# Four-layer attention and expert kernel: the first layer's gate in fewer operations, its row index from two small one-hot tables

## The reference, cut to what matters

```python
K = sigmoid(decay)                                  # attention
states = scan(s = K * s + (kv @ W_in.T + b_in))
y = Z + mean(states @ W_out.T + b_out)
x += (y - mean(y)) / sqrt(var(y) + eps) * gamma + beta

logits = h @ gate_w.T                               # experts
scores = sqrt(softplus(logits))
_, topk_idx = top_k(scores + bias, 6)
topk_w = 1.5 * normalised(scores at topk_idx)
pos = cumsum(onehot(topk_idx)) - 1                  # place in the expert; over 95: dropped
xb[eid, pos] = h
y = (silu(xb @ w_gate) * (xb @ w_up)) @ w_down * topk_w
x += sum of a token's y + shared expert
```

## Time and profile before

| | us |
|---|---|
| median of 3 runs | 1120.19 |
| lowest, highest | 1115.52, 1121.29 |
| the profiled execution | 1117.14 |
| its span (first to last instruction) | 1115.8 |
| mean granted TensorE clock, share of full | 0.948 |
| TensorE busy | 973.4 (87%) |
| VectorE busy | 760.2 (68%) |
| ScalarE busy | 636.0 (57%) |
| GpSimd busy | 532.6 (48%) |

### The profile page before, as it was taken

One profiled execution on the slowest core, in us unless ns is written; L12 is line 12 of the kernel. 1 busy time (PEld: TensorE's weight loads), 2 busy tenths in 40 slices (PEclk: granted clock), 3 DMA queues, 4 the chain that ended last, 5 costly groups with the idle time before them and its releaser, 6 DMA issues.

```text
span 1115.8 us, 18204 instructions
## 1 busy us (share of the span) xinstructions
PE 973.4 (87%) x5865; PEld 797.3 (71%) x5865; DVE 760.2 (68%) x2009; ACT 636.0 (57%) x1808; POOL 532.6 (48%) x584
## 2 busy tenths in 40 slices
PE   5898987189998877769999999999999989998897
PEld 4674654146686656668888888888888778676785
DVE  5685222375657347778899889888987688767344
ACT  2432542002134436759898989899988754653353
POOL 3703677245545363324555555444553145453453
PEclk9788999599998899989999999999999989998999
DMA  9401887830004863020102020101000063005674
GB/s 388 165 12 34 221 210 180 247 78 1 1 1 166 289 218 132 1 61 2 63 1 63 1 63 1 63 1 62 1 24 2 1 202 71 1 1 203 229 273 160
DMA packets 57550, 108.60 MB, mean 97 GB/s; under 512 B 13872, under 2 KB 35504, under 8 KB 55536
## 3 DMA queue, kind: packets, MB, share of 16 engines
q1 hardware_dynamic: 48208, 89.44, 24.1%
q0 software_dynamic: 9248, 18.00, 6.2%
HBM read 78.67 MB, written 27.42 MB: 95 GB/s over the span
## 4 chain that ended last, share of the span: by engine, by line
PE 46%; DVE 20%; ACT 14%; issue 7%; POOL 6%; DMA 5%; SPq 1%; ACTq 0%; DVEq 0%; POOLq 0%
PE bank L200 23%; PE bank L209 8%; ACT a_p L3027 4%; ACT a_p L3035 3%; PE bank L1296 2%; PE bank L2577 2%; DMA sum<-f_ys,f_index 2%; PE bank L1830 2%; ACT a_qt L3010 2%; POOL f_xs L2148 2%; DVE a_qn L2786 2%; DVE stats L239 1%; ACT a_p L2977 1%; PE bank L2627 1%; DVE a_top L2810 1%
## 5 line engine op out<-in xcount | busy, mean ns | idle before, releaser
L3154 POOL TENSOR_TENSOR a_p<-a_p,a_tot 128x128 f32<-128x128 f32 x64 | 50.6, 809 | 183.7 <-DVE a_tot L2758 183.7
L200 PE MATMUL bank<-a_w_high,a_in 128*128 128x256 f32 x384 | 99.0, 295 | 13.8 <-ACT a_p L3035 5.0
L209 PE MATMUL bank<-const 128*128 128x128 f32 x457 | 65.4, 303 | 43.2 <-DVE x L1073 21.7
L200 PE MATMUL bank<-a_w_low,a_in 128*128 128x256 f32 x384 | 94.5, 284 | 0.0
L209 PEld LDWEIGHTS bank<-const 128*128 128x128 f32 x457 | 59.6, 158 | 47.9 <-DVE x L1073 22.1
L200 PEld LDWEIGHTS bank<-a_w_high,a_in 128*128 128x128 f32 x384 | 73.9, 192 | 16.2 <-ACT a_kx L3004 5.5
L3027 ACT ACTIVATE a_p<-bank,a_top 128x256 f32<-128x256 f32 x128 | 59.2, 480 | 31.1 <-DVE a_top L2810 28.7
L200 PEld LDWEIGHTS bank<-a_w_low,a_in 128*128 128x128 f32 x384 | 74.0, 193 | 0.0
L2810 DVE TENSOR_REDUCE a_top<-bank 128x2 f32<-128x512 f32 (+1 forms) x96 | 57.2, 601 | 20.4 <-PE bank L2577 15.7
L200 PE MATMUL bank<-cols,a_kv 128*128 128x256 f32 x256 | 61.9, 384 | 3.6 <-ACT a_kv L2950 3.6
L200 PE MATMUL bank<-a_proj_high,a_catq 128*128 128x256 f32 x256 | 62.2, 284 | 1.2 <-DVE a_catq L2205 0.8
(11 more groups left out here) (437 smaller groups left out, 3087.1 us busy)
## 6 DMA issues: line engine op xcount, KB each, us to landing
experts<-in_experts SPq DMA_DIRECT2D x49, 384.0 KB, 4.5
f_expert<-in_experts SPq DMA_DIRECT2D x31, 384.0 KB, 4.8
third_shelf<-in_groups SPq DMA_DIRECT2D x8, 1024.0 KB, 6.9
f_got<-f_xs SPq DMA_DIRECT2D x10, 516.0 KB, 8.0
third_shelf<-in_groups SPq DMA_DIRECT2D x8, 512.0 KB, 4.2
f_got<-f_ys SPq DMA_DIRECT2D x8, 512.0 KB, 5.1
f_xs<-blank_zero SPq DMA_DIRECT2D x1, 3999.0 KB, 20.8
l_expert<-in_experts SPq DMA_DIRECT2D x10, 384.0 KB, 7.5
```

Source lines behind the costliest of these rows:

```text
L200: ins = pe.matmul(out, lhs, rhs, start=start and n == 0, stop=stop and n == len(pairs) - 1, skip_group_check=shared)
L209: ins = k.pe.transpose(o, i, ident[0:i.shape[0], 0:i.shape[0]])
L3154: g_.tensor_tensor(cross_probs(m, ti), cross_probs(m, ti), over(m.tot[n % 2][:, first:first + HPG], SC), ALU.mult).then_inc(*s["cross_weig ...
```

## The change

In the attention ScalarE makes the sigmoid first, VectorE adds beta itself (two operations over four tiles each, one ahead of `l_keeps` and one after the mean) and finishes all eight tiles; GpSimd is left with the two powers. In the experts' front the rows are shared with ScalarE as in the attention. TensorE does 28 dummy transposes ahead of the turn, 10 instead of 64 behind the key products, and 18 between the place products and the index products as before. ScalarE calls Ln once on one column ahead of the gate's logits, and its four fold copies all come behind the real Ln. The correction of the logarithm is now additive and lies beside ScalarE's Ln. `root_vector` has one Newton step and one step of a higher order, and gives the root itself but for a factor. The mask comes from `max`, a copy of two large values into places 7 and 8 of the best eight, `match_replace`, and one comparison.

The place is held as `code`, the count plus 8 for a chosen expert and 0 for the others, in 16 bits, and split into `low` (three bits) and `high`. Two one-hot tables are compared from them, `low_hot` (32 groups of 8 x 8, 2048 elements) and `high_hot` (32 groups of 12 x 8, 3072 elements). `facts` is `low_hot` times the token's number in two parts, one scaled on VectorE in one operation and one on ScalarE in eight. TensorE multiplies `high_hot` with `facts` in 32 products of 128 columns into one bank; VectorE keeps the diagonal, eight more products with `spread` bring it to 96 x 32, twice, and one reduction makes `number`. The eight grids, the six copies and the table's DMA are gone. The shared expert waits for the index at its third step only. AHEAD is 14, and in GpSimd's loop the scatter now comes ahead of the gather.

```diff
 def layer0_attention_vector(k, m, s, s2):
     normalise_vector(k, s, k.x, k.rows, k.x_ready)
+    def add_beta(half):
...
+        v.tensor_tensor(k.x[:, part, :], k.x[:, part, :], under(w["beta"], HALF), ALU.add).then_inc(*step.one())
+    add_beta(0)
     on.wait_ge(*s["gained"].at(1))
...
+    add_beta(1)
...
-        for c in VECTOR_TILES:
+        for c in range(HALF):
 def layer0_attention_scalar(k, m, s):
-    normalise_scalar(k, s, k.x, k.rows, k.x_ready)
     on.wait_ge(*k.l0_in)
     a.activation(m.keep[:], w["decay"], ACT.Sigmoid).then_inc(*s["gained"].one())
+    normalise_scalar(k, s, k.x, k.rows, k.x_ready)
 def layer0_ffn_tensor(k, m, s):
+    pass_time(k, k.bank[0], 28)
+    turn_rows_tensor(k, s, k.rows, rows_of(s))
...
-    pass_time(k, k.bank[4], 64)
+    pass_time(k, k.bank[4], 10)
     on.wait_ge(*s["mask_ready"].at(1))
...
+    pass_time(k, k.bank[1], 18)
+    on.wait_ge(*s["hot_ready"].at(2))
+    for i in range(NT):
+        on.wait_ge(*s["facts_scaled"].at(i + 1))
+        for c in range(OF):
+            n = i * OF + c
+            ins = pe.matmul(counts[:, c, :], m.high_hot[:, n, :, :].rearrange("p h e -> p (h e)"),
+                            m.facts[:, n, :, :, :].rearrange("p f l e -> p (f l e)"), start=n == 0, stop=n == NT * OF - 1,
+                            skip_group_check=True)
+    ins.then_inc(*s["picked"].one())
+    on.wait_ge(*s["diagonal"].at(1))
+    for low in range(LOW):
+        ins = pe.matmul(k.bank[2][0:CAP, 0:2 * E0], m.spread[:, low, :], m.diagonal[:, :, low, :], start=low == 0,
+                        stop=low == LOW - 1)
+    ins.then_inc(*s["picked"].one())
     on.wait_ge(*k.kq_scaled.at(H1 // 2))
-    pass_time(k, k.bank[PICK_BANKS[0]], 18)
-    for r in range(NT):
-        on.wait_ge(*s["pick_ready"].at(r + 1))
-        for n, bank in enumerate(PICK_BANKS):
-            ins = pe.matmul(k.bank[bank][0:2, :], m.facts[:, r, :], m.picks[r % 2][:, n * BANK:(n + 1) * BANK],
-                            start=r == 0, stop=r == NT - 1)
...
     for r in range(NT + 2):
+        if r == 2:
+            on.wait_ge(*s["indexed"].at(1))
 def layer0_ffn_vector(k, m, s):
+    v.tensor_scalar(t["lost"][:], t["one_plus"][:], 1.0, None, ALU.subtract).then_inc(*step.one())
+    v.tensor_scalar(t["scores"][:], t["small"][:], -0.5, 1.0, ALU.mult, ALU.add).then_inc(*step.one())
+    v.tensor_tensor(t["lost"][:], t["small"][:], t["lost"][:], ALU.subtract).then_inc(*step.one())
+    v.tensor_tensor(t["lost"][:], t["lost"][:], t["scores"][:], ALU.mult).then_inc(*step.one())
     on.wait_ge(*s["gate_log"].at(1))
...
+    root_vector(k, flat_t(t["scores"]), flat_t(t["small"]), flat_t(t["log1p"]), flat_t(t["lost"]))
...
+    v.tensor_copy(m.best[:, :, K0:8], t["biased"][:, :, E0:E0 + 8 - K0]).then_inc(*step.one())
+    for i in range(NT):
+        ins = v.match_replace(m.rest[:, i, :], m.best[:, i, :], t["biased"][:, i, :], TAKEN)
+    v.tensor_scalar(m.mask[:].rearrange("p (t e) -> p t e", t=NT), m.rest[:, :, 0:E0], TAKEN, None,
+                    ALU.is_equal).then_inc(*s["mask_ready"].one())
...
+    v.scalar_tensor_tensor(m.code[:], k.bank[4][:, 0:NT * E0], float(LOW), m.mask[:], ALU.add, ALU.mult).then_inc(
         *s["place_ready"].one())
+    v.tensor_scalar(m.low[:], m.code[:], LOW - 1, None, ALU.bitwise_and).then_inc(*step.one())
+    v.tensor_scalar(m.high[:], m.code[:], 3, None, ALU.logical_shift_right).then_inc(*step.one())
+    v.tensor_tensor(m.low_hot, middle(by_eight(m.low), LOW), around(m.lows), ALU.is_equal).then_inc(
+        *s["hot_ready"].one())
...
+    v.tensor_scalar(m.facts[:, :, 0, :, :].rearrange("p n l e -> p n (l e)"), m.low_hot.rearrange("p n l e -> p n (l e)"),
+                    c["tokpart"], float(NT), ALU.mult, ALU.mult).then_inc(*step.one())
+    v.tensor_tensor(m.high_hot, middle(by_eight(m.high), HIGH), around(m.highs), ALU.is_equal).then_inc(
+        *s["hot_ready"].one())
+    on.wait_ge(*s["picked"].at(1))
+    v.tensor_tensor(m.diagonal[:].rearrange("p n l e -> p (n l) e"), k.bank[1][0:CAP, :].rearrange(
+        "p (n e) -> p n e", e=LOW), under(m.same[:], OF * 2 * LOW), ALU.mult).then_inc(*s["diagonal"].one())
+    on.wait_ge(*s["picked"].at(2))
+    v.tensor_reduce(m.number[:].rearrange("p (c e) -> p c e", c=OF), k.bank[2][0:CAP, 0:2 * E0].rearrange(
+        "p (c f e) -> p c e f", c=OF, f=2), AX.X, ALU.add).then_inc(*step.one())
 def layer0_ffn_scalar(k, m, s):
+    normalise_scalar(k, s, k.x, k.rows, k.x_ready)
     cols_scalar(k, s, k.cols)
+    a.activation(m.warm[:], k.c["ones"][:, 0:1], ACT.Ln)
...
+    on.wait_ge(*s["hot_ready"].at(1))
+    for i in range(NT):
+        part = slice(i * OF, (i + 1) * OF)
+        a.activation(m.facts[:, part, 1, :, :].rearrange("p n l e -> p n (l e)"),
+                     m.low_hot[:, part, :, :].rearrange("p n l e -> p n (l e)"), ACT.Copy, scale=float(i + 1 - NT)).then_inc(
+            *s["facts_scaled"].one())
 def root_vector(k, out, x, value, spare):
+    v.tensor_scalar(bits, x.bitcast(I32), 1, None, ALU.logical_shift_right)
+    v.tensor_scalar(bits, bits, -1, 0x5F375A86, ALU.mult, ALU.add)
+    v.scalar_tensor_tensor(spare, out, -0.5, x, ALU.mult, ALU.mult)
+    v.tensor_tensor(spare, spare, out, ALU.mult)
+    v.scalar_tensor_tensor(out, spare, 1.5008789, out, ALU.add, ALU.mult)
+    v.tensor_tensor(value, value, out, ALU.mult)
+    v.tensor_tensor(out, value, out, ALU.mult)
+    v.scalar_tensor_tensor(spare, out, -10.0 / 3.0, out, ALU.add, ALU.mult)
+    v.scalar_tensor_tensor(out, spare, 5.0, value, ALU.add, ALU.mult)
```

213 lines of the change are left out of this document (99 added, 114 removed).

## The result

Before: median 1119.22 us (1115.52 to 1121.29, four runs). After: median 1081.77 us (1080.43 to 1086.69, four runs). The measured ratio is 0.9677, with a 95% interval of 0.9635 to 0.9719 (the two medians divided give 0.9665): the changed kernel is 3.2% faster. Two later measurements gave 0.970 (0.9678 to 0.9722) and 0.974 (0.9705 to 0.9782). So what is to be explained is 30 to 37 us between the medians where the sum had 26.5.

A forecast was written before the change was run, and what follows sets the result against it. Index readiness and GpSimd's issue time behind it were taken to set layer 1's start. Terms 0.9, 3.9, 8.4, 10.7 and 2.6 sum to 26.5 us off 1117.14, 1090.6, raised to 1092 towards the runs' median; range 1083 to 1098.

The forecast's parts named there:

- the sum: All five parts of the forecast added: 26.5 us off the profiled execution's 1117.14, giving 1090.6.
- part 1: First layer's attention: beta moved from GpSimd to VectorE and sigmoid first on ScalarE gain 0.9 us, bounds 0 to 1.6.
- part 2: Turns and gate: 28 dummy transposes keep TensorE's upper clock through the turns and half the gate, gaining 3.9 us.
- Part 3: Gate end to mask: shorter VectorE work leaves TensorE's key products as the bound, gaining 8.4 us, at most 11.
- Part 4: Mask to index: one-hots and TensorE products replace grids, copies and table transfer; 12.2 us instead of 22.9, gaining 10.7.
- both rivals that turned on it: Index one-hots: one element a cycle, 1096 us, chance 0.20; or costly short runs, 1124 us, chance 0.02.
- Part 5: Behind the index: fourteen gathers instead of 11 ahead of the first scatter, 2.6 us gained, bounds 0.5 to 5.
- The one with the clock and one load less: Gate through index: TensorE keeps 2.4 GHz and Ln's table set serves Exp; 6.4 us more, 1085.5 us, chance 0.22.
- No gain behind the front: Experts' loop: something such as the experts' weights holds it to the old time; 1105 us, chance 0.05.
- short runs cost: Index one-hots: runs of 8 cost 50 ns each, 32 us on the path, slower at 1124 us; chance 0.02.

The follow-up runs named there:

- the 64 dummies: Changed kernel with 64 instead of 10 dummy transposes behind the key products, ahead of the place products; 1090.82 us in one run.
- the first pair: Profiled executions of the first measurement, unchanged edits: kernel before 1117.14 us, changed kernel 1086.69 us.
- the other pair: Later traces of the kernel before and the changed kernel, both unaltered; medians in that measurement 1121.07 and 1086.05 us.
- ten ahead: Changed kernel with AHEAD back at 10 and the gather ahead of the scatter; 83.58 us from first scatter to the sum's load, no whole time given.
- after again: Second trace of the changed kernel, nothing altered; median 1086.05 us in that measurement (four runs).
- the Exp run: Changed kernel with Exp instead of Ln as ScalarE's early warm-up operation; 1084.65 us in one run.
- the control: Changed kernel unaltered, a third time, on the same chip as the three-edit kernel; median 1088.84 us, ratio to before 0.9743.
- the run with three edits: Changed kernel with Exp as warm-up, 2 dummies behind the key products and 45 ahead of the index products; median 1087.41 us, ratio to before 0.9734.

## Why the prediction was right, and where it was not

Its frame held: index time and GpSimd's issue time set layer 1's start, all the gain lies ahead of it, and the delay put in by the 64 dummies arrived there whole. The sum, 26.5, compares with 28.1 and 29.8 at the sum's load, so the direction and nearly the size were right, though the median fell just below the range. Two terms were wrong, in opposite directions: in the first pair part 1 was 2.1 us too small and part 2 2.7 too large, and that they nearly cancel in the sum is luck. And the clock was read as the kernel's, where another execution of the same kernel shows another.

**Part 1, the term that was mis-sized: 0.9 forecast, 3.0 measured.** The sum had "`l_keeps` takes 0.2 and the scans start at 15.7 instead of 16.75" and took the scans themselves for equal. They started at 15.95, and took 1.57 us where they had taken 3.29. The step that failed is the reading of the 1.14 us in the earlier trace rows: as one instruction slowed by a neighbour, where it was an instruction standing until the neighbour's end. Read so, the second addition holds the next instruction behind it as well, and the scans end 2.5 us earlier (15.95 + 1.57 = 17.52 against 16.75 + 3.29 = 20.04); `l_mean_wide` keeps these 2.5. From there to the statistics it takes 15.85 us against 16.36: 0.7 less since VectorE no longer waits within its first additions for TensorE's summary, which kept the upper clock, and 0.2 more for the 16 short operations at the end (7.33 against 7.17). In the other pair the summary is worth 1.6 us (VectorE's waits for it were 1.99 and 0.95 us), and that is why part 1 gained 4.0 there. The sum had no term for it. The Trainium skill ("Trainium Architecture — The Big Picture", "What this means for kernel authors") calls the port pair that VectorE and GpSimd share "an exclusive lock (not a bandwidth split)"; the rows 2015, 2051 and 2030 ns beside additions of 1.99 us agree, and that rule weighed against the earlier trace rows would have mended most of the term. The bounds (0 to 1.6) were worked out without it. Beta on VectorE cost 1.42 and 1.22, the forecast's 1.25 each within 0.2, and the 16 tail operations came at the assumed 0.46.

**Part 2, 3.9 forecast, 1.25 measured (1.7 in the other pair).** "I take the turns at the upper level" was nearly right: 1.2 and 1.6 of the 1.8 us. That held although the dummies ended 2.17 us before the turns and not 1, and one execution (ten ahead) kept only 0.3. "I let the clock fall half way into the gate", with 5.0 us for it, was the failing step: neither kernel ever showed 5.0. The term's own figures, 3.65 to 1.8 and 6.8 to 5.0, also add up to 3.65 and not to 3.9. The gate takes 6.9 us where the clock stays low through it, in two of twelve traces (one of each kernel, both of the first measurement), and 3.7 to 4.1 in the other ten, without dummies as well as with. The term should have held only the turns. What decides the level stays open; products that keep TensorE fuller within the gate weren't tried.

**Part 3, 8.4 forecast, 8.23 measured.** Gate end to place was to take 13.6 us and took 13.70 (64.31 - 50.61), with the mask at 12.8 and TensorE's keys and dummies last, as forecast, at the lower clock of the fold. At the upper clock (after again) the mask comes nearly with them, 59.79 against the place products at 59.94, and the stretch takes 12.98. The prediction had no wait ahead of the key products; at the upper clock there is one, 0.35 us for ScalarE's fold copies. Max8 0.85, the copy 0.18, eight match_replace 1.4 us (0.08 and 0.18 each pair): the assumed pace of `max_index` held. There were two table loads behind the logits, as the row of before had said. The Trainium skill ("ScalarE: Activation LUTs", "Table sets: the hidden batching unit") would have let one set serve both; neither the Ln before Exp (after) nor the Exp before Ln (the Exp run) did so here. The early Ln buys nothing: Exp is loaded behind it, and Ln once more behind that.

**Part 4, 10.7 forecast, 11.35 measured.** From the place products to the index's end: 12.2 forecast, 11.5 here (11.33 to its start). One-hots 1.23 and 1.75 us against 1.15 and 1.7: the pace of the grids (1.69 us for 3072), runs of eight or not, which ends both rivals that turned on it. The index products took 3.49 against 3.4 at the lower clock; at the upper one 1.99, which the forecast had as a bound (1.7). The 0.7 us less are in the small things: the diagonal 0.69 for 0.8, the spread products 0.55 for 0.75, reduce 0.22 for 0.3, and overlaps between short VectorE operations. The new softplus, mask and index (parts 3 and 4, the largest ones) weren't undone in a run of their own; their gain is read from the rows of the traces.

**Part 5, 2.6 forecast, 4.19 and 2.60 measured.** From the first scatter to the sum's load the first pair has 83.55 and 80.88 us, 2.7 less instead of 3.7 (3.5 with the 0.2 for the lone scatters). By itself the exchange is what was forecast: three rounds of a gather and a scatter, 2.99 us each, became three lone scatters of 1.72, which is 3.8 us. Waits among the lone scatters take 1.1 back, the 1.54 us for an expert's result above all; in the control's trace they are longer (one of 1.68 us) and the loop takes 81.60. The first scatter came 18.6 us behind the index's end, not 21.4. Counted from the index's start, as in the landmarks, it is + 18.8, and the granted clock goes with it: + 18.8 in all five traces with the changed front in which the clock stayed at 1.00 until the first scatter, + 20.1 to + 20.5 in the five in which it stood at 0.50 for a part of that time (in the run with three edits as late as 82.3 to 85.5 us, 14 us behind the index). In the two of before it was + 18.2 and + 20.3, with 1.00 and 0.50 behind the index. At the upper clock the change costs 0.6 us here, where the prediction had 1.3; the first pair gains 1.5 us all the same, with 0.50 in its trace of before and 1.00 in that of after.

**The rivals.** The one with the clock and one load less (1085.5) is the nearest to the times, and half of it is true: where the gate keeps the upper clock, the front is 5.9 us earlier (index at 69.95 against 75.83). But that is not the change's doing, since before has it too, and the load is not saved. "No gain behind the front" (1105) and "short runs cost" (1124) are refuted by the sum's load at 175.32 and by 1.23 us for 256 runs.

**Why the median is lower still.** In the first measurement 37.5 us lie between the medians and 30.5 between the profiled executions (1117.14 and 1086.69), of which 28.1 are traced to the stretches above. The clock in the front (up to 6 us at the index) and the rest of the span (7.9 us between traces) move an execution by as much; with the other measurements the difference is 35.0 and 30.0. The other executions of the first measurement have no trace, so how its 37.5 came about is left open.

## What to carry to other kernels

An odd duration of one VectorE instruction beside a GpSimd one may be a wait for that one's end: compare it with the same instruction elsewhere and with where the neighbour ends. If it is, each GpSimd instruction of that kind in the stretch can hold a VectorE instruction, so price the whole of their time there. Not every pair did so here (see below). Then look at who waits behind VectorE: a shorter wait of TensorE also gave back clock. Take a stage's clock from more than one execution before giving its level to a change. And where a serial string is cut on one engine, write the other engine's row beside it: here TensorE's keys and dummies came 0.15 to 1.0 us behind the mask, and 0.4 of 1.3 us saved on ScalarE came through, by way of the copies that TensorE waited for.

## What the runs showed of the hardware

- A scan of 128x64 f32 took 0.26 us; one that met a GpSimd addition of 128x1024 (1.99 us) took 2.02 to 2.05 us, once per addition. VectorE's row scaling (TENSOR_SCALAR, 128x256 f32) wasn't held by GpSimd's own (13.37 to 14.15 us of before): it took 0.41 us from 13.48, as it did from 12.09. GpSimd's took 0.78 us there, and its next one 0.54.
- Sixteen products of 128x256 f32 took 5.41 us behind an idle time of 3.6 to 4.4 us of TensorE (three traces) and 3.72 us behind one of 0.8 to 2.2 us (nine traces).
- The granted clock stayed at 0.50 over 12 us in which TensorE was busy all the time (43.7 to 55.9 us of after), and most of the same instructions ran at 1.00 in other executions. A wait of 3.27 us ahead of the index products was followed by 1.99 us in one execution and 3.49 in another, behind the same instructions.
- A table load of 1.28 us came at each change between Exp and Ln, in either order, and the instruction behind it started 0.01 us after its end (51.53 + 1.28, then 52.82).
- A compare of 16-bit operands with runs of eight took 1.23 us for 2048 elements and 1.75 us for 3072, about as long as the grids with runs of 32 (1.69 us for 3072), and twice as many elements in a us as an f32 addition of 1024 (1.22 us).
